# One attention layer and one feed-forward layer: eight bias additions moved off TensorE, the turn of z put one batch later, the last batch's queues rewritten

## What is computed

```
x = x + layernorm(attention(layernorm(x)))          # 8 batches, 256 tokens, 128 wide
x = x + layernorm(ffn(layernorm(x)))
attention: q, k, v = x @ W_qkv + b_qkv              # 16 heads of 8
           p = softmax(q k^T / sqrt(8) + rel_bias[clip(i - j + 128)])
           out = (p v) @ W_out + b_out
ffn:       h = silu(x w1^T s1) * (x w2^T s2)        # 512 wide
           h = gelu(h h1^T s); h = gelu(h h2^T s); out = h w3^T s3
```

## Time and profile before

| what | value |
|---|---|
| median of 3 runs (lowest, highest) | 290.55 us (290.06 to 291.17) |
| the profiled execution's own time | 290.61 us |
| its span, first to last instruction | 288.8 us |
| around the span | 1.8 us |
| TensorE busy | 267.7 us, 93% |
| VectorE, ScalarE, GpSimd busy | 212.5, 205.2, 102.5 us |
| mean granted TensorE clock | 0.992 of 2.4 GHz |

### The profile page before, as it was taken

The page is one execution under the profiler, slowest core; times in us unless marked ns, Lnnn a source line. Parts: engine busy times, 40 slices in busy tenths (PEclk is TensorE's granted clock), DMA queues, the critical chain, the costliest instruction groups (busy, mean ns, idle before and its releaser), DMA issues.

```text
span 288.8 us, 5174 instructions
## 1 busy us (share of the span) xinstructions
PE 267.7 (93%) x1875; PEld 180.7 (63%) x1875; DVE 212.5 (74%) x442; ACT 205.2 (71%) x316; POOL 102.5 (35%) x107
## 2 busy tenths in 40 slices
PE   7899989899999999999999998999999999999980
PEld 7656646555555555556555554557888888888860
DVE  4576977889789789789788888857654853673675
ACT  2677777785876776785886886767459976896750
POOL 6716000101702603923974985117640202400111
PEclk9999999999999999999999999999999999999996
DMA  6979505322221262560221200000000000010012
GB/s 159 339 231 142 184 5 183 129 65 90 64 84 41 74 194 103 179 210 21 75 78 36 78 0 3 1 3 1 0 2 0 0 0 2 0 36 2 2 36 77
DMA packets 21356, 21.17 MB, mean 73 GB/s; under 512 B 3664, under 2 KB 18768, under 8 KB 21072
## 3 DMA queue, kind: packets, MB, share of 16 engines
q1 hardware_dynamic: 20464, 20.53, 24.4%
q10 hardware_dynamic: 864, 0.27, 0.4%
HBM read 14.90 MB, written 5.64 MB: 71 GB/s over the span
## 4 chain that ended last, share of the span: by engine, by line
PE 68%; DVE 16%; ACT 8%; issue 5%; DMA 1%; POOL 1%; ACTq 0%; POOLq 0%; DVEq 0%
PE place L1449 11%; PE place L1450 11%; PE place L1252 10%; PE pv L1304 7%; DVE mx L692 6%; PE place L1244 5%; ACT ring L1016 4%; PE place L1278 4%; DVE place L699 3%; PE place L1203 2%; PE misc L1315 2%; PE place L1289 2%; PE misc L1182 2%; PE pv L1450 2%; PE pv L1449 2%
## 5 line engine op out<-in xcount | busy, mean ns | idle before, releaser
L692 DVE TENSOR_REDUCE mx<-place 128x4 f32<-128x1024 f32 x64 | 78.3, 1223 | 16.2 <-PE place L1252 14.9
L517 POOL TENSOR_TENSOR rstd<-mv,mhalf 128x2 f32<-128x2 f32 (+1 forms) x26 | 20.9, 806 | 145.8 <-DVE mv L624 145.8
L1016 ACT ACTIVATE ring<-place 128x1024 f32<-128x1024 f32 x64 | 65.7, 1028 | 6.4 <-PE place L1289 3.1
L1252 PE MATMUL place<-room,identr 128*128 128x512 f32 x128 | 47.0, 448 | 0.0
L1023 ACT COPY place<-raw 128x1024 f32<-128x1024 f32 x37 | 37.8, 1024 | 11.7 <-DVE mx L692 11.7
L1449 PE MATMUL place<-room,w_hi 128*128 128x512 f32 (+1 forms) x116 | 44.7, 387 | 0.7 <-DVE room L825 0.7
L1450 PE MATMUL place<-room,w_hi 128*128 128x512 f32 (+1 forms) x116 | 44.1, 383 | 0.0
L1304 PE MATMUL pv<-ring,vx 128*9 128x256 f32 x512 | 33.6, 380 | 0.4 <-ACT ring L1016 0.4
L825 DVE TENSOR_TENSOR room<-ring,room 128x512 fp32r<-128x512 f32 x32 | 21.3, 690 | 17.1 <-ACT room L1104 17.1
L1244 PE MATMUL place<-room 33*128 33x256 f32 x256 | 28.4, 298 | 4.9 <-ACT ring L1016 4.8
L1278 PE MATMUL place<-room 33*128 33x256 f32 x256 | 31.7, 328 | 1.4 <-DVE place L699 1.1
(11 more groups left out here) (141 smaller groups left out, 434.4 us busy)
## 6 DMA issues: line engine op xcount, KB each, us to landing
raw<-ext SPq DMA_DIRECT2D x8, 384.0 KB, 6.8
room<-q_parts SPq DMA_DIRECT2D x48, 64.0 KB
room<-k_parts SPq DMA_DIRECT2D x48, 64.0 KB
w_lo<-h SPq DMA_DIRECT2D x2, 1024.0 KB, 5.6
q_parts<-w_hi SPq DMA_DIRECT2D x4, 256.0 KB, 3.0
k_parts<-w_hi SPq DMA_DIRECT2D x2, 512.0 KB, 3.4
xs<-x SPq DMA_DIRECT2D x3, 256.0 KB, 6.1
w_lo<-w SPq DMA_DIRECT2D x3, 256.0 KB, 2.8
```

What stands on the lines that cost most here:

```text
L517: nc.gpsimd.tensor_tensor(rstd[:, at:at + width], mv[:, at:at + width, 1], mhalf[:, 0:width], ALU.pow).then_inc(rstd_set, 1)
L692: nc.vector.tensor_reduce(mx[:, s // RPAIRS, :, :, s % RPAIRS].rearrange("p i k -> p k i"), max_tile(b * PAIRS + s)[:, :, :].rearrange("p ...
L1016: nc.scalar.activation(probs[:, s % PRING, :, :, :].rearrange("p k j n -> p (k j n)"), score_tile(b * PAIRS + s)[:, :, :].rearrange("p k n ...
L1252: last = mm(max_tile(b * PAIRS + s)[:, half, :], identr[:, :], windows(table_hi[:, 2 * s + half, :], 0, P, 2, S), start=False, stop=True, ...
```

## The change

1. `BY_PE` is empty: in batches 0 to 6 ScalarE copies pair 7's bias as it does those of pairs 0, 1, 3, 4 and 6. In its queue this copy stands ahead of the exponential of pair 6.
2. `z` lies in two places in turn. `norm_T`, `keep_zT` and `z_low` of batch b - 2 (not b - 1) stand at s = 7 of batches 2 to 5. Batch 6 does two: z of batch 4 at s = 6 and of batch 5 at s = 7. TensorE's wait for `minus_max` that stood ahead of `norm_T` at s = 7 in batches 5 and 6 is now at s = 6; in batch 5 two unread matmuls follow it.
3. The last batch is written out: TensorE adds the bias of pairs 3 and 6, VectorE writes 1, 2, 4, 5 and 7, ScalarE 0. Each step's scores stand ahead of the transposes. `maxima_T` now stands ahead of `weighted(6, 3)` and waits for the `z_low` of batch 5. VectorE writes pair 1's bias ahead of that `z_low`.
4. `zeros` and `ones` share one tile, set by two memsets in a row, and GpSimd makes two low tables in place of one.

```diff
--- before.py
+++ after.py
-BY_PE = (7,)
+BY_PE = ()
 BY_DVE = (2, 5)
-LAST_BY_DVE = (1, 2, 4, 5, 6)
-LOW_AT_SLOT = {2 * s + k: 2 * i + k for i, s in enumerate(BY_PE) for k in range(2)}
+LAST_BY_PE = (3, 6)
+LAST_BY_DVE = (1, 2, 4, 5, 7)
+LOW_PAIRS = BY_PE + tuple(s for s in LAST_BY_PE if s not in BY_PE)
...
-        zeros = sb("zeros", [2 * PAIRS, S], F32R)
-        ones = sb("ones", [2 * PAIRS, S], F32R)
+        zeros_and_ones = sb("zeros_and_ones", [32 + 2 * PAIRS, S], F32R)
+        zeros, ones = zeros_and_ones[0:2 * PAIRS, :], zeros_and_ones[32:32 + 2 * PAIRS, :]
...
-        z = y_and_z[:, TPB * D:2 * TPB * D].rearrange("p (t d) -> p t d", t=TPB)
+        z_odd = sb("z_odd", [P, TPB * D])
+        z_places = (y_and_z[:, TPB * D:2 * TPB * D], z_odd[:, :])
+        z = [z_places[b % 2].rearrange("p (t d) -> p t d", t=TPB) for b in range(B)]
...
+        def by_pe(b):
+            return BY_PE if b + 1 < B else LAST_BY_PE
         def by_act(b):
-            return tuple(s for s in range(PAIRS) if s not in BY_PE + by_dve(b))
+            return tuple(s for s in range(PAIRS) if s not in by_pe(b) + by_dve(b))
...
             nc.gpsimd.memset(mhalf[:, :], -0.5).then_inc(const_set, 1)
+            nc.gpsimd.memset(zeros_and_ones[:, :].bitcast(F32), 1.0).then_inc(ones_set, 1)
+            pool.wait_ge(ones_set, 1)
             nc.gpsimd.memset(zeros[:, :].bitcast(F32), 0.0).then_inc(ones_set, 1)
-            nc.gpsimd.memset(ones[:, :].bitcast(F32), 1.0).then_inc(ones_set, 1)
...
+            for s in LOW_PAIRS:
+                table_low(s)
...
-                if b > 0:
-                    dve.wait_ge(zT_ready, b)
+                if b > 1:
+                    dve.wait_ge(zT_ready, b - 1)
                 for t in range(TPB):
-                    last = normalize(z[:, t, :], xs[:, b * TPB + t, :], t)
+                    last = normalize(z[b][:, t, :], xs[:, b * TPB + t, :], t)
...
-            for b in range(B):
+            for s in range(2):
+                if s in BY_DVE:
+                    dve.wait_ge(raw_in[s], 16)
+                    write_bias(s)
+            for b in range(B - 1):
                 for s in range(PAIRS):
-                    if b + 1 < B:
-                        maxima(b + 1, s)
-                    if b + 1 == B and s + 1 in by_dve(b) and s == 0:
-                        write_bias(b * PAIRS + s + 1)
+                    maxima(b + 1, s)
                     if s + 2 in by_dve(b):
                         if b == 0:
                             dve.wait_ge(raw_in[s + 2], 16)
+                        write_bias(b * PAIRS + s + 2)
+                    elif (s + 2) % PAIRS < 2 and (s + 2) % PAIRS in BY_DVE and b + 2 < B:
                         write_bias(b * PAIRS + s + 2)
                     if b == 0:
                         if s in (2, 3):
...
                     if b > 0:
                         if s in (1, 2):
                             weigh(b - 1, s - 1)
-                        if s == 3 and b + 1 == B:
-                            largest_low()
                         if s == 4:
                             attn_moments(b - 1)
-                            if b + 1 == B:
-                                any_low()
                         if s == 5:
                             residual(b - 1)
                         if s == 6:
...
                                 q_and_k_low(4, b - 2)
                             if b == 4:
                                 keep_v(4)
-                        if s == 7 and b + 1 < B:
-                            z_low(b - 1)
+                            if b + 2 == B:
+                                z_low(b - 2)
+                        if s == 7:
+                            if b + 2 == B:
+                                write_bias((b + 1) * PAIRS + 1)
+                                z_low(b - 1)
+                            elif b > 1:
+                                z_low(b - 2)
+            first = (B - 1) * PAIRS
+            write_bias(first + 2)
+            weigh(B - 2, 0)
+            write_bias(first + 4)
+            write_bias(first + 5)
+            weigh(B - 2, 1)
+            write_bias(first + LAST_BY_DVE[-1])
+            largest_low()
+            attn_moments(B - 2)
+            any_low()
+            residual(B - 2)
+            second_norm(B - 2)
...
             write_bias(0)
-            for b in range(B):
+            for b in range(B - 1):
                 for s in range(PAIRS):
                     ahead = b * PAIRS + s + 1
-                    if ahead < B * PAIRS and ahead % PAIRS in by_act(ahead // PAIRS):
+                    if ahead % PAIRS in by_act(ahead // PAIRS):
                         write_bias(ahead)
                     probabilities(b, s)
                     if s == 0:
...
                             q_and_k_high(3, s - 2)
                     if s == 3 and b > 0:
                         keep_onT(b - 1)
-                    if s == 5 and b + 1 < B:
+                    if s == 5:
                         minus_max(b + 1, 0)
...
                             keep_xT(4)
+                            for u in range(1, 3):
+                                act.wait_ge(parts_out[u], PARTS_OUT)
                         if b in (2, 3):
                             q_and_k_high(4, b - 2)
-                    if s == 7 and b > 0 and b + 1 < B:
-                        if b == 1:
-                            for u in range(1, 3):
-                                act.wait_ge(parts_out[u], PARTS_OUT)
-                        keep_zT(b - 1)
+                        if b + 2 == B:
+                            keep_zT(b - 2)
+                    if s == 7:
+                        if b + 2 == B:
+                            keep_zT(b - 1)
+                        elif b > 1:
+                            keep_zT(b - 2)
+            last = B - 1
+            probabilities(last, 0)
+            keep_weighted(last - 1, GROUPS - 1)
+            minus_max(last, 1)
+            probabilities(last, 1)
+            probabilities(last, 2)
+            keep_weighted(last, 0)
+            probabilities(last, 3)
+            probabilities(last, 4)
+            keep_weighted(last, 1)
+            keep_onT(last - 1)
+            probabilities(last, 5)
+            probabilities(last, 6)
+            keep_weighted(last, 2)
+            probabilities(last, 7)
             nc.scalar.activation(table_loaded[:, :], mhalf[:, 0:1], ACT.Silu)
             keep_weighted(B - 1, GROUPS - 1)
...
             pe.wait_ge(qk_lo_set, 3)
             v(2)
-            for b in range(B):
-                more = b + 1 < B
+            for b in range(B - 1):
                 for s in range(PAIRS):
-                    if more or s not in BY_PE:
-                        scores(b, s)
-                    if s == 6 and 1 <= b <= 4:
+                    scores(b, s)
+                    if s == 6 and b > 0:
                         pe.wait_ge(mrow_set, b * RANGES + 3)
                         if b == 1:
                             x_T(4)
...
                             q_and_k(4, b - 2)
                         if b == 4:
                             v(4)
-                    if more:
-                        max_scores(b + 1, s)
-                        max_bias(b + 1, s)
-                    if s in BY_PE and more:
+                        if b == 5:
+                            stream(misc, blank, blank, BLANKS[0])
+                        if b + 2 == B:
+                            norm_T(b - 2)
+                    max_scores(b + 1, s)
+                    max_bias(b + 1, s)
+                    if s in BY_PE:
                         score_bias(b, s)
-                    if s + 1 in BY_PE and not more:
-                        scores(b, s + 1)
-                        score_bias(b, s + 1)
                     if s == 0:
                         if b > 0:
                             weighted(b - 1, GROUPS - 1)
-                        if b > 1:
-                            pe.wait_ge(z_lo_set, b - 1)
                         if b == 0:
                             pe.wait_ge(qk_lo_set, 4)
+                        if b > 2:
+                            pe.wait_ge(z_lo_set, b - 2)
                         maxima_T(b, 1)
-                    else:
-                        if s % 2 == 0:
-                            weighted(b, s // 2 - 1)
+                    elif s % 2 == 0:
+                        weighted(b, s // 2 - 1)
                     if b > 0:
                         if s == 1:
                             pe.wait_ge(mrow_set, b * RANGES + 2)
...
                             if b == 1:
                                 pe.wait_ge(out_w_in, 32)
                             project(b - 1)
-                            if not more:
-                                pe.wait_ge(y_read, b)
-                                pe.wait_ge(w_low_top_set, 2)
-                                mm(misc[0:1, 0:P], w_low_top[:, :], ident[:, :], start=True,
```

(43 more changed lines are left out.)

21 lines of the change are left out of this document (11 added, 10 removed).

## The result

| | before | after |
|---|---|---|
| median (lowest, highest), 8 runs each | 290.68 us (290.06, 291.17) | 293.67 us (291.71, 295.73) |
| ratio, 95% interval | | 1.0104 [1.006, 1.0148] |
| profiled execution, its span | 290.61, 288.8 us | 295.25, 293.5 us |
| its mean granted clock | 0.992 | 0.959 |
| mean granted clock in the 8 runs | | 0.959 to 0.979 |

The changed kernel is slower by 1.0%, where I forecast 289.8 us and no difference, and it lies outside my range. Its runs also spread over 4 us, where those of before spread over 1.1. The profiled execution, at 295.25 us, is among the longest of them.

A forecast was written before the change was run, and what follows sets the result against it. The prediction took each batch as a loop of three legs, on TensorE, VectorE and ScalarE, not TensorE alone. Its sum was 290.6 - 2.1 (batches 0 to 6) + 1.3 (joint and last batch) = 289.8 us, range 286.9 to 291.9.

The forecast's parts named there:

- rival 4: Joint of batches 6 and 7: thin TensorE work lets the clock fall, 8 us cost 4, giving 293.8 us; chance 0.10.
- my own rule from the tail: Read after the last matmul: the clock falls from 2.4 to 1.2 GHz after a few idle us.
- TensorE loses 7.0 us of work: Batches 0 to 6: seven sets of four bias matmuls go, 1.0 us each; worth only the exponential's wait.
- Batches 1 to 4: Pair 7's exponential stops waiting for bias matmuls: gain 1.16 us in batches 1 to 3, 0.95 in batch 4.
- Batch 0: ScalarE's queue brings pair 7's exponential at 53.2 against 53.25, so gain 0.
- Rival 3: Batches 1 to 4: ScalarE takes TensorE's place, the 2.1 us are given back, 291.9 us; chance 0.11.
- Batches 5 and 6: Maxima of step 6 and the leg that starts from them don't move: cost 0, loops still 20.0 us.
- Rival 2: Every batch: TensorE is the bound, as its 93% busy say; each gives 1.0, 284.9 us; chance 0.06.
- The joint and last batch: Batches 6 and 7: the late z_low of batch 5 delays maxima_T and the feed-forward start; +1.3 us.
- Rival 1: Last batch: the waits of 1.29 us vanish and it ends 1.4 us early, 287.1 us; chance 0.18.
- z one batch later: Batches 1 to 5: removes norm_T's wait for second_norm, its work lies where TensorE waits anyway; 0.
- The set-up: Start: two memsets under 0.1 us, and the second low table falls into GpSimd's idle time; 0.

The follow-up runs named there:

- e2: e1 plus four more unread matmuls at each of steps 6 and 7 of batch 0; median 289.96 us, ratio 0.9959.
- e4: Kernel before, with only pair 7's bias moved from TensorE to ScalarE in batches 1 to 4; median 289.54 us, ratio 0.9946.
- e5: e4 plus six unread matmuls of zeros at step 7 of batches 1 to 4; median 288.49 us, ratio 0.9919.
- e3: Changed kernel with the joint and the last batch put back into the order of before; median 290.73 us, ratio 0.9983.
- e10: Changed kernel with z_low of batch 5 ahead of pair 1's bias on VectorE, no unread matmuls added; median 293.4 us, ratio 1.0133.
- e1: Changed kernel plus 14 unread matmuls of zeros ahead of maxima_T(7, 1); median 289.97 us, ratio 0.9959.
- e8: e7 with z_low of batch 5 ahead of pair 1's bias on VectorE, and 4 for 14 unread matmuls; median 287.85 us, ratio 0.9901.
- e7: Changed kernel plus six unread matmuls at step 7 of batches 0 to 6 and 14 ahead of the last maxima_T; median 288.79 us, ratio 0.9935.

## Why the prediction was wrong

The step that failed is the clock's term in the sum 290.6 - 2.1 + 1.3: it was put at nothing, and the fall stood only in rival 4, at 0.10 and outside the range. In the runs the fall costs 5.2 us of the median (293.67 against 288.5 at full clock) and 6.5 us of the profiled execution. The mechanism of rival 4 was right, and so was its place for the longest fall. That its 293.8 us meets the median of 293.67 is luck: it added 4 us for 8 us of low clock to a base of 289.8 us that was 1.3 us too high, had no fall in the batches, and the profiled fall at the joint was 13.6 us long and cost 5.1. Two sentences of it misled me. "The clock is at full everywhere" was taken as evidence for the changed kernel, though it is a property of a queue that still held the matmuls to be removed. And "it falls from 2.4 to 1.2 GHz after a few idle us", read from the end of the kernel, where nothing at all ran, bounded the risk to places with a long gap. The Trainium skill ("TensorE: Matmul & The Clock Gate", Part 1), which I quoted there, has activity release the throttled state. That work can be too thin without any long gap is my reading of it; e2 agrees with it, with no gap over 0.66 us ahead of its first fall, and my own rule from the tail doesn't.

**The bias matmuls, priced at their wait.** "TensorE loses 7.0 us of work" was right, and I priced what it took off the path. Nothing in the sum stood for what the work did beside that. e4 against e5 measures it: the same edit with 24 unread matmuls added is 1.05 us faster in the median, and 4 us in the worst run. Rival 4 had the fall only at the joint; in the profiled runs it also came at the end of batch 0 (after, e3, e10), 1 (e2, e3, e4), 2 (e2) and 5 (e1). One stretch of 3.4 us cost its loop 1.4 to 1.5 us (after, e4, e10, e1), two of them 3.0 us (e3, loops 0 and 1), and the two of e2 6.1 us.

**Batches 1 to 4: -2.1 forecast, -2.4 measured** (0.55 + 0.43 + 0.43 + 1.00). The idle time ahead of the exponential, read from the earlier trace rows, is a fair price to within 0.1 us each.

**Batch 0: 0 forecast, -0.46 measured.** I laid ScalarE's four instructions end to end by their durations, 1.02 + 1.02 + 0.37 + 1.02. ScalarE in batch 0 of e8:

```profile
49.74 1.02 ACT L1052 COPY place<-raw 128x1024 f32<-128x1024 f32 x1 [0.68 <-DVE mx L703]
50.69 1.02 ACT L1045 ACTIVATE ring<-place 128x1024 f32<-128x1024 f32 x1
...
51.61 0.36 ACT L1057 COPY oT<-pv 128x256 f32<-128x256 f32 x1
51.86 1.03 ACT L1052 COPY place<-raw 128x1024 f32<-128x1024 f32 x1
52.81 1.04 ACT L1045 ACTIVATE ring<-place 128x1024 f32<-128x1024 f32 x1
```

From start to start they take 0.95, 0.92, 0.25 and 0.95, 3.07 us for 3.43. That is 0.36 of the 0.46 us. Rival 3, ScalarE as the next bound, didn't come, as loops 1 to 4 kept their gain. But TensorE does wait for ScalarE now: the 0.66 us of e2's rows above, where the bias matmuls stood, end with ScalarE's copy of the next pair 0's bias.

**Batches 5 and 6: 0, and 0 measured** in loop 5 (19.98 in both). Rival 2 is out: the page's 93% were not the bound.

**The joint and last batch: +1.3 forecast, +0.74 measured at full clock** (0.49 + 0.25), inside my bounds but near the lower, the count from start to start. I had `maxima_T` 0.77 us later (180.05 for 179.28), and it came 0.49 later. From there to the feed-forward I had 15.3 us by the busy row and 14.4 from start to start, and it took 14.82, between the two. I had also misread what the 1.29 us of waits before were for. In the timeline of before, TensorE waits there 0.25 and 0.52 us for VectorE (`weigh` and the read of `misc`) and 0.49 us for ScalarE's copy from `pv`, and for no bias: that wait, 0.40 us, ends at 180.06, where the window begins.

```profile
180.06 0.50 PE L1278 MATMUL place<-room 33*128 33x256 f32 x4 [0.40 <-DVE place L699]
...
184.36 0.44 PE L1322 MATMUL misc<-ident,on 128*128 128x128 f32 x2 [0.25 <-DVE on L711]
...
187.81 0.38 PE L1412 MATMUL misc<-ident,w_low_top 128*1 128x128 f32 x2 [0.52 <-DVE y_and_z L720]
...
191.94 0.98 PE L1170 MATMUL pv<-blank 128*128 128x256 f32 x6 [0.49 <-ACT oT L1028]
```

With the change 0.31 us is left (e7), for `minus_max` ahead of `back(6, 0)`, which I had at 0.45. `z_low` of batch 5 as the one that TensorE waits for was right, and e8 shows the price: 0.83 us for two VectorE instructions in the wrong order. Rival 1, a shorter last batch, didn't come: from the last batch's first scores to the first product it was 16.51 us before (177.34 to 193.85), 17.14 in e7 (174.69 to 191.83) and 22.30 in the profiled execution of the change.

**z one batch later: 0, and 0 measured** in batches 2 to 4, by e4 and e5 against the full change. The set-up: 0; `maxima_T(0, 1)` starts at 34.6 in before and e8.

With 0.10 put on the clock for the joint alone and none for the batches, 0.18 on the slower side was too little, and the range should have reached 294.
